# Cross attention of a two-layer block: two row normalisations move from VectorE to ScalarE, with their shift computed on GpSimd

## The chip, the cores and the metric

The kernel runs on one core of a Trainium2 chip. The metric is the device time of one execution in microseconds, of which the median over several runs is compared. In the names of the profile PE is TensorE (PEld its weight loads), DVE is VectorE, ACT is ScalarE, POOL is GpSimd and SP the engine that issues the DMAs.

## The reference, cut to what matters

The input `x` has 32 batches of 64 rows of 256 values, 2,048 rows in all. Four sublayers follow each other, each adding its output to `x`: linear attention, a mixture-of-experts feed-forward layer, softmax cross attention over `ctx_2048`, and a dense feed-forward layer. The change lies in the third. What it computes, of each row:

```
x = x + L1_xattn(_layernorm(x), ctx_2048, mask, Wq, bq, Wk, bk, Wv, bv, Wo, bo, ln_gamma, ln_beta, residual_scale)

_layernorm(x):                 (x - mean) / sqrt(var + 1e-5)
in L1_xattn:                   q, k, v projections, scores, clip, softmax, probs @ v -> ctx
delta = clip(residual_scale, 0, 0.3) * (ctx @ Wo.T + bo)
delta = (delta - mean(delta)) / sqrt(var(delta) + 1e-5) * ln_gamma + ln_beta
```

So each row is normalised twice in this layer: `x` before the query projection, and the delta before it is scaled by gamma and added to `x`.

## The kernel before, in words

The 2,048 rows are 16 tiles of 128 rows; `x` stays in SBUF for the whole run. The program has four stages, one for each sublayer. Every engine has its own instruction list, written out by hand, and the lists meet only through semaphores: `after(eng, sem, t, back)` waits until step `t - back` of `sem` is done. An engine works strictly in the order of its list, so that a waiting instruction holds back all that stands behind it.

In a stage each engine's list is a row of slots, one for each tile (`slots`, L99). Slot `s` holds work on several tiles at once: `s.tile(2)` is the tile two ahead, `s.tile(-2)` the one two behind. The first and last slots are unrolled and those between are a loop of two slots, an even and an odd one. The two differ: the queries and keys of two tiles are computed in the even slot.

In the cross attention stage (`slot2` of each engine) this happens in a slot `s`:

- PE: in an even slot the keys of two tiles (12 products), in each slot the values of tile `s` (L1342), the transpose of the attention output of tile `s-2` (L1357), in an even slot the queries of two tiles and the weighted values of tile `s-1` (L1303), then the output projection of tile `s-2` (helper lines L251 to L253), the transpose of the normalised `x` of tile `s+2` (L294), and the scores (L1326). An odd slot has the scores first and the weighted values last, behind L294.
- DVE: statistics of `x` of tile `s+2` (L266, L270), the low half of the transposed attention output (L1002), the values (L926), the normalisation of `x` of tile `s+2` (`ln_norm_step`, L286), the normalisation of the delta of tile `s-3` (`delta_norm`, L948), clipping of scores (L985), the softmax sums (L961 to L974), the delta of tile `s-2` (L935) with its statistics (L939, L943), and the low half of the transposed `x` (L307).
- ACT: in an even slot the keys (L659, four instructions), the high half of the transposed attention output (L669), in an odd slot the exponentials of the scores (L650), in an even slot the queries (L678, four), then the high half of the context (L338) and of the transposed `x` (L301), and in an odd slot L650 again.
- POOL: variance plus epsilon and its power of -1/2 of `x` of tile `s+2` (L276, L279: the reciprocal deviation, `rstd`), the low half of the context (L345), gamma, beta and the residual of tile `s-3` (L506, L508, L510), and the reciprocal deviation of the delta of tile `s-2` (L515, L518, `rstd2`).

Both normalisations are one DVE instruction each, with two values per partition as operands: subtract the mean, multiply by the reciprocal deviation. At the end of the stage slots 16 and 17 already hold work of the last sublayer: the first six of the eight feature blocks of its first group of tiles (L1287 on PE, L635 on ACT with the Gelu table), its transposes (L1272) and their copies (L645); the last two blocks follow in `slot3`.

## Time and profile before

| | us |
|---|---|
| median of 3 runs | 524.58 |
| lowest and highest run | 524.57, 527.5 |
| span of the profiled execution | 524.4 |
| PE busy in it | 485.8 (93%) |
| DVE busy | 383.4 (73%) |
| ACT busy | 217.7 (42%) |
| POOL busy | 155.0 (30%) |

The span runs from the first to the last instruction of one profiled execution; the profile gives no other time of it, and it stands 0.2 us below the median of the runs. A busy share is a mean over four stages with different limits. The cross attention stage covers roughly 327 to 453 us. Where a time point is given below, it is counted from the start of the span.

### The profile page before, as it was taken

Reading aid. Unit: us, or ns where it says so; the run is one execution under the profiler, and the core shown is the slowest. Engines: PE = TensorE matmul, PEld = TensorE weight load, DVE = VectorE, ACT = ScalarE, POOL = GpSimd, SP = SyncE. Lnnn points to the kernel's source line nnn. Section 1 sums busy time; section 2 is a strip of 40 time slices with the busy share of each in tenths; the row PEclk is TensorE's granted clock in tenths of the full one; section 3 lists DMA queues with packets and bytes.
Section 4 is the critical chain, followed back from the end, with each engine's and each line's share of the span. In section 5 each row is a group of like instructions: output and inputs, shape, how many; then the busy total and the mean of one; then the engine's idle time right before and its main releaser. Section 6 shows DMA issues by size and latency. Waiting matters only on the chain. (4 is left out here: it accounts for less than half of the span.)

```text
span 524.4 us, 11913 instructions
## 1 busy us (share of the span) xinstructions
PE 485.8 (93%) x3744; PEld 426.8 (81%) x3744; DVE 383.4 (73%) x1159; ACT 217.7 (42%) x501; POOL 155.0 (30%) x287
## 2 busy tenths in 40 slices
PE   3789999998999999999999999998899889699996
PEld 2567777776888888888888888887888878699995
DVE  5578777777777777777777776788788698666542
ACT  4444555542333333333333335553555444454540
POOL 3434444432111111111111121246455465632100
PEclk9999999999999999999999999998999799899999
DMA  8522222111000000000000000000000000000111
GB/s 279 166 57 62 58 58 58 38 41 45 16 17 16 15 15 15 15 15 15 15 15 15 16 11 11 21 22 22 12 19 20 10 1 2 0 22 22 40 40 42
DMA packets 15088, 18.06 MB, mean 34 GB/s; under 512 B 2001, under 2 KB 14546, under 8 KB 15058
## 3 DMA queue, kind: packets, MB, share of 16 engines
q1 hardware_dynamic: 15058, 17.69, 11.3%
q8 instruction: 15, 0.25, 0.2%
q14 instruction: 15, 0.12, 0.1%
HBM read 15.59 MB, written 2.10 MB: 34 GB/s over the span
## 5 line engine op out<-in xcount | busy, mean ns | idle before, releaser
L251 PE MATMUL PS<-wfh,arena_r 128*128 128x256 f32 (+2 forms) x352 | 121.3, 345 | 1.4 <-DVE arena_r L855 1.4
L252 PE MATMUL PS<-wfl,arena_r 128*128 128x256 f32 (+2 forms) x352 | 116.1, 330 | 0.0
L253 PE MATMUL PS<-wfh,arena_r 128*128 128x256 f32 (+2 forms) x352 | 116.1, 330 | 0.0
L276 POOL TENSOR_TENSOR ve<-mv,eps 128x1 f32<-128x1 f32 x64 | 12.8, 201 | 221.3 <-DVE mv L270 221.0
L251 PEld LDWEIGHTS PS<-wfh,arena_r 128*128 128x128 f32 x352 | 66.6, 189 | 10.1 <-DVE arena_r L855 4.8
L253 PEld LDWEIGHTS PS<-wfh,arena_r 128*128 128x128 f32 x352 | 66.6, 189 | 7.2
L252 PEld LDWEIGHTS PS<-wfl,arena_r 128*128 128x128 f32 x352 | 66.6, 189 | 4.9
L592 ACT ACTIVATE arena_r<-PS 128x512 fp32r<-128x512 f32 (+1 forms) x48 | 25.1, 526 | 62.2 <-PE PS L1187 62.2
L597 ACT ACTIVATE arena_f<-PS 128x512 f32<-128x512 f32 (+1 forms) x48 | 25.3, 527 | 53.0 <-PE PS L253 52.8
L286 DVE TENSOR_SCALAR arena_f<-x,mv,rstd 128x256 f32 (+1 forms) x48 | 37.0, 771 | 13.7 <-POOL rstd L279 13.3
L874 DVE SCALAR_TENSOR_TENSOR arena_f<-arena_f,tiny,PS 128x128 f32<-128x128 f32 x144 | 43.2, 356 | 0.6
L635 ACT ACTIVATE arena_f<-PS,cols 128x256 f16<-128x256 f32 x64 | 26.6, 471 | 32.4 <-PE PS L1287 30.1
L855 DVE TENSOR_TENSOR arena_r<-PS,arena_r 128x512 fp32r<-128x512 f32 (+1 forms) x48 | 28.2, 588 | 16.0 <-ACT arena_r L592 16.0
L279 POOL TENSOR_TENSOR rstd<-ve,mhalf 128x1 f32<-128x1 f32 x64 | 35.4, 552 | 8.1 <-POOL ve L276 6.0
L345 POOL TENSOR_TENSOR arena_r<-ctx_raw,arena_r 128x256 fp32r<-128x256 f32 x32 | 24.6, 770 | 43.2 <-ACT arena_r L338 43.1
L251 PE MATMUL PS<-w0h,arena_r 128*128 128x256 f32 (+1 forms) x96 | 35.0, 364 | 1.3 <-DVE arena_r L812 0.7
L1287 PE MATMUL PS<-arena_r,w1h 128*128 128x256 f32 x128 | 33.3, 298 | 2.0 <-ACT arena_r L645 1.0
L294 PE MATMUL PS<-ident,arena_f 128*128 128x128 f32 x96 | 19.6, 287 | 16.5 <-DVE arena_f L286 12.6
L358 POOL TENSOR_TENSOR wfl<-raw,wfh 128x482 f32 (+1 forms) x16 | 19.6, 1225 | 49.5 <-ACT wfh L352 49.5
L301 ACT ACTIVATE arena_r<-PS 128x256 fp32r<-128x256 f32 x48 | 18.3, 382 | 37.3 <-PE PS L294 34.3
L1287 PE MATMUL PS<-arena_r,w1l 128*128 128x256 f32 x128 | 32.8, 293 | 0.0
L1303 PEld LDWEIGHTS PS<-arena_f 128*64 128x64 f32 x512 | 30.4, 148 | 2.5 <-issue 1.5
(137 smaller groups left out, 1245.2 us busy)
## 6 DMA issues: line engine op xcount, KB each, us to landing
ctx_raw<-in_ctxT SPq DMA_DIRECT2D x32, 128.0 KB, 2.1
raw<-in_w_ffn SPq DMA_DIRECT2D x16, 241.0 KB, 2.6
raw<-in_w_l SPq DMA_DIRECT2D x16, 192.0 KB, 2.4
out<-arena_f SPq DMA_DIRECT2D x8, 256.0 KB, 2.2
x<-in_x SPq DMA_DIRECT2D x1, 1792.0 KB, 9.9
raw<-in_w_l SPq DMA_DIRECT2D x2, 512.0 KB, 5.0
rows<-in_rows SPq DMA_DIRECT2D x1, 640.0 KB, 6.1
x<-in_x SPq DMA_DIRECT2D x1, 256.0 KB, 2.8
```

What stands on the lines that cost most here:

```text
L251: nc.tensor.matmul(out_ap, lh, rh, start=first, stop=False)
L252: nc.tensor.matmul(out_ap, lh, rl, start=False, stop=False)
L253: return nc.tensor.matmul(out_ap, ll, rh, start=False, stop=last)
L279: nc.gpsimd.tensor_tensor(rstd[:, r:r + 1], ve[:, r:r + 1], mhalf[:, 0:1], ALU.pow).then_inc(ln_rstd, 1)
L286: nc.vector.tensor_scalar(dst[:, r, :], x[:, at_tile(t), :], mv[:, r, 0:1], rstd[:, r:r + 1], ALU.subtract, ALU.mult).then_inc(xn_ready, 1)
L592: nc.scalar.activation(fTh[:, at], PS[:, bank, 0:at.stop - at.start], ACT.Copy).then_inc(S1["hT_hi"], 1)
L597: nc.scalar.activation(fth[:, at], PS[:, bank, 0:at.stop - at.start], ACT.Tanh, scale=0.5).then_inc(S1["tanh"], 1)
L635: nc.scalar.activation(md16[:, r, n, :], PS[:, M_H + n // 2, (n % 2) * D:(n % 2 + 1) * D], ACT.Gelu, bias=cols[:, 2 * KC + n:2 * KC + n + ...
L855: nc.vector.tensor_tensor(fTl[:, at], PS[:, bank, 0:at.stop - at.start], fTh[:, at].bitcast(F32), ALU.subtract).then_inc(S1["hT_lo"], 1)
L874: last = nc.vector.scalar_tensor_tensor(out=fh[:, c], in0=fa[:, c], scalar=weight, in1=PS[:, bank, u:u + c.stop - c.start], op0=ALU.mult, ...
L1287: last = nc.tensor.matmul(PS[:, M_H + n // 2, (n % 2) * D:(n % 2 + 1) * D], m0w[w][:, c, n * P:(n + 1) * P], mX[r][:, c, :], start=c + w = ...
L1303: last = nc.tensor.matmul(PS[SEQ * b:SEQ * (b + 1), X_C, g * PVC:(g + 1) * PVC], pp[r][:, b, i, (c * 2 + j) * SEQ:(c * 2 + j + 1) * SEQ], ...
```

## The change

Both normalisations of the stage become ACT activations, `Identity` with a scale (the reciprocal deviation) and a bias (the shift) per partition: `x * rstd + shift`. The shift is `0 - mean * rstd`, and POOL computes it with two instructions on 128x1 behind each reciprocal deviation. DVE loses its two instructions per slot. The normalisation of `x` in the other stages stays on DVE; tiles 0 to 2 of this stage are normalised in the stage ahead and stay there too.

```diff
+        shift, shift2 = sb("shift", [P, 2]), sb("shift2", [P, 2])
+        zero = sb("zero", [P, 1])
...
+        def ln_shift_step(pool, t, r):
+
+            after(pool, ln_rstd, t, 0, 2 * TILES)
+            nc.gpsimd.tensor_tensor(shift[:, r:r + 1], mv[:, r, 0:1], rstd[:, r:r + 1], ALU.mult).then_inc(ln_mr, 1)
+            after(pool, ln_mr, t, 0, -3)
+            nc.gpsimd.tensor_tensor(shift[:, r:r + 1], zero[:, 0:1], shift[:, r:r + 1], ALU.subtract).then_inc(ln_shift, 1)
+
+        def ln_scale_step(act, t, r, dst):
+
+            after(act, ln_shift, t, 0, -3)
+            after(act, xT_psum, t, 2, 2 * TILES)
+            nc.scalar.activation(dst[:, r, :], x[:, at_tile(t), :], ACT.Identity, bias=shift[:, r:r + 1],
+                                 scale=rstd[:, r:r + 1]).then_inc(xn_ready, 1)
...
             def slot2(s):
                 if tile := normalised_in(s):
                     ln_rstd_step(pool, 2, *tile)
+                    ln_shift_step(pool, *tile)
...
                     nc.gpsimd.tensor_tensor(rstd2[:, r:r + 1], ve2[:, r:r + 1], mhalf[:, 0:1],
                                             ALU.pow).then_inc(S2["d_rstd"], 1)
+                    after(pool, S2["d_rstd"], t)
+                    nc.gpsimd.tensor_tensor(shift2[:, r:r + 1], mv2[:, r, 0:1], rstd2[:, r:r + 1],
+                                            ALU.mult).then_inc(S2["d_mr"], 1)
+                    after(pool, S2["d_mr"], t)
+                    nc.gpsimd.tensor_tensor(shift2[:, r:r + 1], zero[:, 0:1], shift2[:, r:r + 1],
+                                            ALU.subtract).then_inc(S2["d_shift"], 1)
...
                     nc.scalar.activation(aTh[:, r, :], PS[:, X_T, D:2 * D], ACT.Copy).then_inc(S2["cnT_hi"], 1)
+                if tile := s.tile(-3):
+                    t, r = tile
+                    after(act, S2["d_shift"], t)
+                    after(act, x_done[2], t, 2)
+                    nc.scalar.activation(dn[:, r, :], dl[:, r, :], ACT.Identity, bias=shift2[:, r:r + 1],
+                                         scale=rstd2[:, r:r + 1]).then_inc(S2["dn"], 1)
                 if s.ring == 1 and s.tile(-1):
                     exp_scores(*s.tile(-1))
+                if ahead := normalised_in(s):
+                    ln_scale_step(act, *ahead, xn if s.tile(2) else mx16)
                 if s.ring == 0 and s.tile(0):
...
-            slots(act, TILES, 0, TILES + 1, slot2)
+            slots(act, TILES, 0, TILES + 2, slot2)
...
-            def delta_norm(t, r):
-                after(dve, S2["d_rstd"], t)
-                after(dve, x_done[2], t, 2)
-                nc.vector.tensor_scalar(dn[:, r, :], dl[:, r, :], mv2[:, r, 0:1], rstd2[:, r:r + 1],
-                                        ALU.subtract, ALU.mult).then_inc(S2["dn"], 1)
...
                 if here:
                     values(*here)
-                if ahead:
-                    ln_norm_step(dve, 2, *ahead, xn if s.tile(2) else mx16)
-                if tile := s.tile(-3):
-                    delta_norm(*tile)
```

What this does to the lists is seen in the loop of the stage. ACT, the even slot, from the keys to the context, before:

```order
L659 ACTIVATE arena_f<-PS,bkm,headmask 128x2x2x64 x4
L118 REGISTER_ALU x2
L669 ACTIVATE arena_r<-PS 128x256
L678 ACTIVATE raw<-PS,bqm,headmask 128x2x2x64 x4
L330 ISA
```

And ACT at the same place in the changed kernel (L684 is the keys, L694 the high half of the attention output, L711 the queries):

```order
L684 ACTIVATE arena_f<-PS,bkm,headmask 128x2x2x64 x4
L118 REGISTER_ALU x2
L694 ACTIVATE arena_r<-PS 128x256
L118 REGISTER_ALU x2
L699 ACTIVATE arena_f<-arena_f,shift2,rstd2 128x256
L118 REGISTER_ALU
L295 ISA
L295 ACTIVATE arena_f<-x,shift,rstd 128x256
L711 ACTIVATE raw<-PS,bqm,headmask 128x2x2x64 x4
L347 ISA
```

Both normalisations (L699 of the delta, L295 of `x`) now stand between the attention output and the queries, and so ahead of the context step that POOL waits for.

POOL in the loop, from the residual of tile `s-3` into the next slot, before:

```order
L510 TENSOR_TENSOR x<-x,arena_f 128x256
L118 REGISTER_ALU
L515 TENSOR_TENSOR ve2<-mv2,eps 128x1
L518 TENSOR_TENSOR rstd2<-ve2,mhalf 128x1
L118 REGISTER_ALU
L276 TENSOR_TENSOR ve<-mv,eps 128x1
L118 REGISTER_ALU
```

And POOL at the same place in the changed kernel:

```order
L529 TENSOR_TENSOR x<-x,arena_f 128x256
L118 REGISTER_ALU
L534 TENSOR_TENSOR ve2<-mv2,eps 128x1
L537 TENSOR_TENSOR rstd2<-ve2,mhalf 128x1
L540 TENSOR_TENSOR shift2<-mv2,rstd2 128x1
L543 TENSOR_TENSOR shift2<-zero,shift2 128x1
L118 REGISTER_ALU
L279 TENSOR_TENSOR ve<-mv,eps 128x1
L118 REGISTER_ALU
L282 TENSOR_TENSOR rstd<-ve,mhalf 128x1
L287 TENSOR_TENSOR shift<-mv,rstd 128x1
```

Four instructions on one column are new in each slot: two for the delta ahead of the next tile's reciprocal deviation, and two (L287 and L289) behind it.

## Rows read from the trace of the kernel before

**Rows 1.** The page: granted TensorE clock in 40 slices of the span, tenths of full speed.
```profile
PEclk9999999999999999999999999998999799899999
```

**Rows 2.** Windows: stretch, length, busy us (instructions) of PE, PEld, DVE, ACT, POOL, granted clock, DMA share, GB/s.
```profile
360.00:364.00 4.00, 3.02 (x32) 2.65 (x31) 3.89 (x9) 1.63 (x4) 2.87 (x4) 0.73 0.13 33
...
408.00:412.00 4.00, 2.94 (x29) 2.41 (x27) 3.89 (x8) 1.55 (x4) 2.68 (x5) 0.70 0.11 33
...
456.00:460.00 4.00, 2.98 (x17) 2.62 (x15) 2.92 (x5) 1.38 (x4) 3.24 (x6) 0.50 0.00 0
```

**Rows 3.** Timeline of PE in an odd slot: start us, us, engine, line, [idle before].
```profile
392.27 0.39 PE L251 MATMUL PS<-w1h,arena_r 128*128 128x256 f32 x1 [0.62 <-DVE arena_r L1002]
...
394.31 0.44 PE L294 MATMUL PS<-ident,arena_f 128*128 128x128 f32 x2 [1.06 <-DVE arena_f L286]
```

**Rows 4.** Timeline of DVE, an even slot's normalisation, then an odd slot's work.
```profile
386.94 0.41 DVE L286 TENSOR_SCALAR arena_f<-x,mv,rstd 128x256 f32 x1
...
392.14 1.19 DVE L926 TENSOR_TENSOR arena_f<-PS,rows 64x128 f32<-64x128 f32 x4
393.36 0.90 DVE L286 TENSOR_SCALAR arena_f<-x,mv,rstd 128x256 f32 x1
```

**Rows 5.** Timeline of ACT, one even slot.
```profile
383.05 1.93 ACT L659 ACTIVATE arena_f<-PS,bkm,headmask 128x256 f32<-128x256 f32 x4 [1.16 <-PE PS L253]
384.86 0.39 ACT L669 ACTIVATE arena_r<-PS 128x256 fp32r<-128x256 f32 x1
385.34 1.93 ACT L678 ACTIVATE raw<-PS,bqm,headmask 128x256 f32<-128x256 f32 x4
387.15 0.43 ACT L338 ACTIVATE arena_r<-ctx_raw 128x256 fp32r<-128x256 f32 x1
```

**Rows 6.** Timeline of POOL, from the even slot's context step into the odd slot.
```profile
387.73 0.72 POOL L345 TENSOR_TENSOR arena_r<-ctx_raw,arena_r 128x256 fp32r<-128x256 f32 x1 [2.61 <-ACT arena_r L338]
...
391.10 0.55 POOL L518 TENSOR_TENSOR rstd<-ve,mhalf 128x1 f32<-128x1 f32 x1
391.99 0.19 POOL L276 TENSOR_TENSOR ve<-mv,eps 128x1 f32<-128x1 f32 x1 [0.34 <-DVE mv L270]
392.34 0.55 POOL L279 TENSOR_TENSOR rstd<-ve,mhalf 128x1 f32<-128x1 f32 x1 [0.16 <-POOL ve L276]
393.38 0.72 POOL L345 TENSOR_TENSOR arena_r<-ctx_raw,arena_r 128x256 fp32r<-128x256 f32 x1 [0.49 <-ACT arena_r L338]
```

**Rows 7.** Groups by line: two operands per partition on ACT.
```profile
L678 ACT ACTIVATE raw<-PS,bqm,headmask 128x256 f32<-128x256 f32 x25 | 12.1, 562 | 1.2 <-PE PS L253 1.0
```

**Rows 8.** Timeline of DVE, the normalisation of other odd slots.
```profile
360.47 0.82 DVE L286 TENSOR_SCALAR arena_f<-x,mv,rstd 128x256 f32<-128x256 f32 x1
...
378.14 0.89 DVE L286 TENSOR_SCALAR arena_f<-x,mv,rstd 128x256 f32 x1
...
408.59 0.90 DVE L286 TENSOR_SCALAR arena_f<-x,mv,rstd 128x256 f32 x1
...
426.62 0.90 DVE L286 TENSOR_SCALAR arena_f<-x,mv,rstd 128x256 f32 x1
```

**Rows 9.** Timeline of ACT and POOL in slots 16 and 17, where the last sublayer begins.
```profile
446.59 0.55 POOL L279 TENSOR_TENSOR rstd<-ve,mhalf 128x1 f32<-128x1 f32 x1
...
456.49 0.55 POOL L518 TENSOR_TENSOR rstd<-ve,mhalf 128x1 f32<-128x1 f32 x1
...
456.47 0.84 ACT L635 ACTIVATE arena_f<-PS,cols 128x256 f16<-128x256 f32 x2 [4.85 <-PE PS L1287]
457.20 0.66 ACT L645 ACTIVATE arena_r<-PS 128x256 fp32r<-128x256 f16 x2
```

**Rows 10.** Timeline of PE at the same place.
```profile
452.46 0.39 PE L251 MATMUL PS<-w1h,arena_r 128*128 128x256 f32 x1 [1.70 <-DVE arena_r L1002]
...
454.39 0.55 PE L1287 MATMUL PS<-arena_r,w1h 128*128 128x256 f32 x1 [0.95 <-DVE arena_f L935]
...
457.91 0.58 PE L1287 MATMUL PS<-arena_r,w1h 128*128 128x256 f32 x1 [1.02 <-ACT arena_r L645]
```

4 lines of the change are left out of this document (3 added, 1 removed).

## The prediction, made before the changed kernel ran

> **What bounds the kernel now.** I read the page first. Its busy shares give PE 93%, but that is a mean over four stages, and the change touches one of them. The line of the granted TensorE clock [rows 1] shows tenths below 9 in three places behind the middle, all at or behind 340 us: inside the cross attention stage and at its end. The windows there give the level: 0.50, the 1.2 GHz level of the two, and a mean of 0.73 or 0.70 where a window of 4 us holds the change of level [rows 2]: a clock that halves at about 361.8 and 409.6. So PE is the bound where it runs, and the stage loses time in two ways: PE pauses, and PE at half clock.
>
> The timeline of PE in the stage shows where it pauses: in the odd slots alone, once for 0.62 us until DVE has split the attention output (L1002) and once for 1.06 us until the normalised `x` of the tile two ahead is there (L286) [rows 3]. What ends the second pause is the object of this change. DVE starts L286 late, because the values (L926, four of them) stand ahead of it and end at about 393.33, and L286 then takes 0.90 us, where the same instruction in the even slot takes 0.41 [rows 4]. POOL had `rstd` ready at 392.34 + 0.55 = 392.89 [rows 6], so POOL had 0.44 us in hand there. It had 0.34 us more in front of L276, where it waited for the statistics [rows 6].
>
> The odd slot's L286 starts at 360.47, 378.14, 393.36, 408.59 and 426.62 [rows 8]. A pair of slots takes 15.22 us, and 17.67 and 18.03 us in the two pairs that hold a stretch at half clock. Such a stretch costs 2.45 and 2.81 us, 2.6 in the mean.
>
> **What the change does, part by part.** *DVE.* It loses L286 and L948 in each slot, some 0.41 + 0.41 us in an even and 0.90 + 0.4 in an odd one. In the even slot nobody waits for them. In the odd slot the end of L286 releases PE, so what counts is when the ACT instruction that takes its place ends.
>
> *One ACT normalisation.* Before, ACT has no instruction with two operands per partition that reads SBUF. The nearest row is L678, with both a bias and a scale per partition, from PSUM: 0.562 us [rows 7]. Four in a row take 1.93 us [rows 5], so one more behind another adds (1.93 - 0.562) / 3 = 0.456. Below, 0.41 (what DVE takes for it) would be a gain of 0.15 on it; above, 0.65. I take 0.56, since two operands per partition are what the two forms share. The Trainium skill, "ScalarE: Activation LUTs", "What ACT_TABLE_LOAD costs", has 186 ns plus 0.833 ns for each column plus some 93 ns for each such operand, which for 256 columns gives an estimate of 0.585 us; by it each pair of slots would be 0.05 to 0.07 us longer, 0.4 in the sum.
>
> *ACT in the even slot.* The keys, the attention output (L669, 384.86) and the queries (L678, 385.34) stand close: with the overlap of 0.10 that neighbours show, L678 could have started at 385.15, so ACT has 0.19 us in hand [rows 5]. Two normalisations put there take 0.91, so the queries and the context step behind them (L338, 387.15) come 0.72 later. POOL's L345 waits for exactly that: it had idled 2.61 us for it [rows 6].
>
> *POOL.* From L345 on POOL runs with next to no gap: L506, L508, L510, L515, L518, up to 391.65. The chain therefore moves 0.72 as a whole. Then come two instructions for `shift2`. One on a single column takes 0.19 us as L276 does, and with its wait for its predecessor 0.27 (L279 in the unrolled part starts 0.27 behind L276, 0.35 in the loop [rows 6]); two cost 0.54. They eat the 0.34 in hand. So `rstd` is ready at 392.89 + 0.72 + 0.54 - 0.34 = 393.81, and the shift at 394.35. ACT starts at 394.40 and ends at 394.96, where L286 ended at 394.26. PE's transposes come 0.70 us later, and so does all that follows, the next even slot's keys included, which releases the ACT chain of the next pair: the loop is closed, so that the 0.70 is paid again in each pair.
>
> Odd slots with this wait: those of tiles 1, 3, ..., 13, seven. 7 x 0.70 = **4.9 us**. With 0.35 for each new POOL instruction instead of 0.27 it is 0.32 more in each pair, 2.2 us in all; I keep that for the range.
>
> *The end of the stage.* In slot 16 the two normalisations stand ahead of the load of the Gelu table, which followed L669 directly. The shift that the second needs is there at 446.59 + 0.55 + 0.54 = 447.68 [rows 9], in time, so they cost 2 x 0.46 = 0.92. The last output projection (452.46), which hangs through L1002 on ACT's work behind the Gelus, moves with it. The hidden products at 454.39 waited for DVE's delta (L935) [rows 10], which stood behind L286; I take 0.25 for that wait, which goes, so they come at about 455.05. Behind them POOL has, for the last tile's delta, to run L506 to L510, L515, L518 and the two new ones. It ended L518 at 456.49 + 0.55 = 457.04 [rows 9]. Now two more pairs of shift instructions stand ahead of the chain, where POOL had waited for L948; I take 0.2 for what of them shows: 457.04 + 0.2 + 0.54 = 457.8 for the last shift. Now it matters who waits: before, this went to DVE; now ACT's last normalisation stands ahead of the two late Gelus (456.47 before) and the copies (457.20, 0.66 long). They end at 457.85 + 0.46 + 0.73 + 0.66 = 459.7 instead of 457.86 [rows 9], and PE's next products (457.91 [rows 10]) wait for the copies: **1.9 us**. Behind that the last stage is PE alone on the chain of waits, and gives nothing back.
>
> *The clock.* Both stretches at half clock in the loop begin within 0.6 us behind the end of an odd slot's pause: the pause ends with L286 at 361.29 and 409.49 [rows 8], the clock halves at about 361.8 and 409.6 [rows 2]. At the other five odd slots the same pause passes at full clock. With 1.06 + 0.70 us the second pause of every odd slot is longer by two thirds, and PE's share of the work in it lower. I expect more of the odd slots to be followed by 1.2 GHz: the trace has two in seven, all seven is the end of the scale. I take five, three more than now: 3 x 2.6 = **7.8 us**. No row says which; zero and five more (13 us) are the bounds.
>
> **The sum.** 4.9 + 1.9 + 7.8 = 14.6 us on the profiled span of 524.4 gives 539.0; the median of the runs stands 0.2 above that span, so **539 us**, +2.8%.
>
> **Rivals.** *The lists get longer, but the clock doesn't fall more often.* For it: five of seven pauses of 1.06 us passed without a fall. Against it: all of them grow. 4.9 + 1.9 = 6.8, with the falls at other places: 531.5, and 533.7 with the dearer POOL steps. Chance 0.20.
>
> *Slack takes it.* If ACT's and POOL's new work finds room that the one pair read here doesn't show (DVE is freed of 1.3 us in the odd slot, so that L270 and L1002 may come earlier and with them L276), only the end's 1.9 and part of the rest is left: 526.5. Against it: in the pair read POOL waited for ACT in the even slot, and DVE has no part in that. Chance 0.10, all of it within 1%.
>
> *DVE was held up by POOL, and that is what ends.* The odd slot's L286 overlaps POOL's L345 (393.38 to 394.10) and ends 0.16 behind it, after 0.90 us; alone it takes 0.41 [rows 4, 6]. On ACT it would take 0.56 and end at 393.36 + 0.56 = 393.92, 0.34 earlier, if the shift is there by 393.3. Then 7 x 0.34 = 2.4 us are gained; the pause until L1002 (0.62) goes too, since the odd slot's DVE list is shorter, another 0.5 x 7 = 3.5; and with shorter pauses the two half-clock stretches may go, 5.2. That gives 524.6 - 11 = 513.5 at best, 518.7 without the clock. It decides as soon as ACT's two insertions delay L345 by less than 0.2 us instead of 0.72. Against it is the 0.19 us in hand. The Trainium skill, "SBUF — State Buffer", "Who interferes with whom", has it that a VectorE tensor_scalar in its two-port mode and a GpSimd instruction shut each other out for a whole instruction, while ScalarE waits for nobody; by that rule moving the normalisation off DVE is right in itself, and the trace's 0.90 against 0.41 agrees. Chance 0.06.
>
> That leaves 0.64 for the forecast.
>
> **Numbers.** About 1% (5.2 us) is what a measurement of this kernel can tell from no change. Slower by more than that, above 529.8: forecast and first rival, 0.84. Within 1%: 0.10. Faster: 0.06. Range: the lower end reaches into the slack case at 529; the upper one is five more falls and dearer POOL steps, 524.6 + 4.9 + 2.2 + 1.9 + 13 = 546.6, so 547. About 0.1 is left out below and 0.05 above.
>
> **What would show it.** In the profile after: POOL's context step in even slots starts 0.7 us later behind the queries; POOL runs without a gap from there to the odd slot's second shift instruction; PE's transposes in odd slots wait for the ACT normalisation, about 1.8 us instead of 1.06; pairs without a fall take some 15.9 us; ACT's new instructions take 0.56; DVE idles more and is waited for less; stretches at 0.50 follow most odd slots. I am wrong if the pair stays at 15.2 (slack), if the transposes wait for ACT not because of POOL's shift but of the exponentials ahead of it, or if the half-clock stretches stay at three, in which case the sum is 7.8 too high.

## The result and the profile after

| | before | changed |
|---|---|---|
| median, us | 524.58 | 543.88 |
| lowest and highest run, us | 524.45, 527.5 (4 runs) | 540.23, 545.66 (4 runs) |
| span of the profiled execution, us | 524.4 | 543.7 |
| its mean granted clock | 0.978 | 0.948 |

The change makes the kernel slower: the ratio is 1.034, 95% interval 1.029 to 1.039. The four runs of the changed kernel took 545.5, 545.7, 542.2 and 540.2 us, the last two at a higher mean clock (0.955 and 0.961). The profiled one is the first, so its span of 543.7 is one of the two longest. The ratios here and below leave out runs more than 1.5% above the fastest of their kernel, which are three of one kernel (the normalisation of `x` on ACT in odd slots, 530.8 to 531.5 us).

The time of a run stands 1.8 us above the span of its own execution (545.53 and 543.7). By that the span of 524.4 before belongs to an execution of about 526.2 us, an estimate. So the difference of the two spans, 19.3 us, compares two executions in the upper part of their ranges; that the medians also differ by 19.3 is a coincidence.

In the program names after the change, L295 is the ACT normalisation of `x`, L699 that of the delta, L287 and L289 are POOL's shift of `x`, L540 and L543 its shift of the delta. L311 is the transpose of `x` on PE, L254 the first product of the output projection, L675 the exponentials, L355 and L362 the context step on ACT and POOL. The trace writes `shift` and `rstd` for `shift2` and `rstd2` too.

First the page: busy time and share by engine, and the granted clock in 40 slices.

```profile
PE 499.0 (92%) x3744; PEld 440.0 (81%) x3744; DVE 368.7 (68%) x1126; ACT 233.5 (43%) x534; POOL 168.1 (31%) x354
...
PEclk9989999999999999999999997998878878789999
```

ACT and POOL have grown by 15.8 and 13.1 us, DVE has lost 14.7. None of them is near full. What has changed in shape is the clock line: against three slices below 9 in the second half of [rows 1], there are now ten. (A slice of 8 between 27 and 41 us lies in the first stage; the transposes at the start of the cross attention stage come 0.36 us later than before, 327.03 against 326.67.) Three windows of 4 us from there give the level: 0.50, the 1.2 GHz level, and in two of them PE is busy for all of the 4 us.

```profile
404.00:408.00 4.00, 4.00 (x19) 4.00 (x20) 1.67 (x7) 1.05 (x3) 2.74 (x9) 0.50 0.00 0
457.00:461.00 4.00, 4.00 (x33) 3.93 (x32) 2.09 (x9) 0.90 (x1) 1.86 (x6) 0.50 0.01 4
472.00:476.00 4.00, 2.50 (x12) 2.17 (x12) 2.18 (x6) 0.70 (x2) 2.98 (x7) 0.50 0.00 0
```

Over the whole of 320 to 500 us the mean granted clock was 0.94 before and is 0.86 now. A mean of 0.94 over 180 us is 2 x 0.06 x 180 = 22 us at half clock; 0.86 is 50 us. The columns are as in [rows 2].

```profile
320.00:500.00 180.00, 164.24 (x1627) 152.70 (x1626) 133.62 (x382) 88.90 (x190) 79.08 (x155) 0.94 0.05 16
```
```profile
320.00:500.00 180.00, 157.47 (x1466) 146.21 (x1465) 107.90 (x320) 96.55 (x203) 87.51 (x209) 0.86 0.05 13
```

Next the timeline of PE at the odd slots' transposes of `x`, which answers to [rows 3]. In brackets stands the pause ahead of it and what ended it.

```profile
332.74 0.44 PE L311 MATMUL PS<-ident,arena_f 128*128 128x128 f32 x2 [1.70 <-ACT arena_f L295]
...
350.06 0.41 PE L311 MATMUL PS<-ident,arena_f 128*128 128x128 f32 x2 [0.84 <-issue]
...
365.92 0.44 PE L311 MATMUL PS<-ident,arena_f 128*128 128x128 f32 x2 [2.39 <-ACT arena_f L295]
...
380.07 0.39 PE L254 MATMUL PS<-w1h,arena_r 128*128 128x256 f32 x1 [0.26 <-DVE arena_r L1027]
...
383.33 0.44 PE L311 MATMUL PS<-ident,arena_f 128*128 128x128 f32 x2 [2.28 <-ACT arena_f L295]
...
400.97 0.44 PE L311 MATMUL PS<-ident,arena_f 128*128 128x128 f32 x2 [2.49 <-ACT arena_f L295]
...
419.36 0.69 PE L311 MATMUL PS<-ident,arena_f 128*128 128x128 f32 x2 [1.70 <-ACT arena_f L295]
...
438.39 0.44 PE L311 MATMUL PS<-ident,arena_f 128*128 128x128 f32 x2 [2.48 <-ACT arena_f L295]
...
455.97 0.29 PE L1293 MATMUL PS<-ident,raw 128*128 128x128 f16 x2 [0.66 <-ACT raw L295]
```

The pause for `x` was 1.06 us and is 2.3 to 2.5 in four of the six that ACT ends, and 1.70 in the first and at 419.36; the smaller one before it has shrunk from 0.62 to 0.26. One pair, 350.06 to 365.92, shows no loss of clock: it takes 15.86 us, where the same pair took 14.93 before. The others take 17.3 to 19.0.

ACT shows what the pause consists of. Here is its odd slot:

```profile
381.11 0.60 ACT L699 ACTIVATE arena_f<-arena_f,shift,rstd 128x256 f32<-128x256 f32 x1 [1.97 <-POOL shift L543]
381.62 1.04 ACT L675 ACTIVATE arena_f<-arena_f 128x1024 f32<-128x1024 f32 x1
382.68 0.60 ACT L295 ACTIVATE arena_f<-x,shift,rstd 128x256 f32 x1
```

And POOL from its context step in an even slot to the shifts of the odd one, one pair of slots later; it answers to [rows 6]:

```profile
394.25 0.73 POOL L362 TENSOR_TENSOR arena_r<-ctx_raw,arena_r 128x256 fp32r<-128x256 f32 x1 [4.34 <-ACT arena_r L355]
...
397.63 0.55 POOL L537 TENSOR_TENSOR rstd<-ve,mhalf 128x1 f32<-128x1 f32 x1
398.25 0.19 POOL L540 TENSOR_TENSOR shift<-mv,rstd 128x1 f32<-128x1 f32 x1
398.52 0.19 POOL L543 TENSOR_TENSOR shift<-zero,shift 128x1 f32<-128x1 f32 x1
```

From the context step on, POOL has no gap to L543 but 0.2 us ahead of L529. ACT idles for that shift of the delta, 1.97 us in the slot shown and 2.02 a pair later, and all that stands behind L699 in its list has idled with it: the exponentials and the normalisation of `x` that PE needs. The three follow each other without a gap. This closes the ring that the prediction drew: the even slot of ACT (answering to [rows 5]) holds both normalisations between keys and queries, and its context step, which POOL waits for, comes later.

```profile
388.78 1.94 ACT L684 ACTIVATE arena_f<-PS,bkm,headmask 128x256 f32<-128x256 f32 x4 [3.65 <-PE PS L256]
390.60 0.40 ACT L694 ACTIVATE arena_r<-PS 128x256 fp32r<-128x256 f32 x1
390.86 0.62 ACT L699 ACTIVATE arena_f<-arena_f,shift,rstd 128x256 f32<-128x256 f32 x1
391.35 0.61 ACT L295 ACTIVATE arena_f<-x,shift,rstd 128x256 f32 x1
391.85 1.95 ACT L711 ACTIVATE raw<-PS,bqm,headmask 128x256 f32<-128x256 f32 x4
393.64 0.45 ACT L355 ACTIVATE arena_r<-ctx_raw 128x256 fp32r<-128x256 f32 x1
```

The context step comes 4.86 us behind the keys, before 387.15 - 383.05 = 4.10 [rows 5].

At the end of the stage, answering to [rows 10], the last output projection, the first late products and the products behind the copies:

```profile
470.11 0.39 PE L254 MATMUL PS<-w1h,arena_r 128*128 128x256 f32 x1 [2.35 <-DVE arena_r L1027]
472.20 0.55 PE L1308 MATMUL PS<-arena_r,w1h 128*128 128x256 f32 x1 [0.67 <-DVE arena_f L968]
477.23 0.58 PE L1308 MATMUL PS<-arena_r,w1h 128*128 128x256 f32 x1 [2.53 <-ACT arena_r L670]
```

The last of them stands 19.3 us later than in [rows 10], and the span is 19.3 us longer. So all but 0.4 us of the loss is made between 327 and 477 us, and nothing is given back behind it.

### The profile page after: what moved, and what is told of

It reads as the page before. It is cut to its first block, busy times and chain, and to the rows that moved or that the text cites. A ratio compares the mean times of both kernels' runs of the same rounds, so it can differ in the third digit from the quotient of the medians.

```text
span 543.7 us, 11987 instructions
## 1 busy us (share of the span) xinstructions
PE 499.0 (92%) x3744; PEld 440.0 (81%) x3744; DVE 368.7 (68%) x1126; ACT 233.5 (43%) x534; POOL 168.1 (31%) x354
## 3 DMA queue, kind: packets, MB, share of 16 engines
q1 hardware_dynamic: 15058, 17.69, 10.7%
## 4 chain that ended last, share of the span: by engine, by line
PE 67%; POOL 10%; issue 8%; ACT 7%; DVE 4%; DMA 1%; ACTq 0%; POOLq 0%; SPq 0%; DVEq 0%
PE PS L254 15%; PE PS L255 14%; PE PS L256 14%; PE PS L1308 6%; PE PS L1417 6%; PE PS L1324 3%; PE PS L1208 3%; ACT raw L711 2%; POOL wfl L375 2%; PE PS L311 2%; DVE arena_f L303 1%; POOL rstd L282 1%; POOL arena_f L527 1%; POOL arena_r L362 1%; POOL arena_f L525 1%
## 5 line engine op out<-in xcount | busy, mean ns | idle before, releaser
L254 PE MATMUL PS<-wfh,arena_r 128*128 128x256 f32 (+2 forms) x352 | 121.3, 345 | 1.4 <-DVE arena_r L888 1.4
L254 PEld LDWEIGHTS PS<-wfh,arena_r 128*128 128x128 f32 x352 | 66.5, 189 | 10.1 <-DVE arena_r L888 4.8
L362 POOL TENSOR_TENSOR arena_r<-ctx_raw,arena_r 128x256 fp32r<-128x256 f32 x32 | 24.9, 777 | 53.7 <-ACT arena_r L355 53.7
L311 PE MATMUL PS<-ident,arena_f 128*128 128x128 f32 x96 | 19.8, 289 | 23.0 <-ACT arena_f L295 13.0
L1308 PE MATMUL PS<-arena_r,w1h 128*128 128x256 f32 x128 | 35.4, 310 | 3.2 <-ACT arena_r L670 2.5
L303 DVE TENSOR_SCALAR arena_f<-x,mv,rstd 128x256 f32 (+1 forms) x35 | 28.3, 810 | 13.8 <-POOL rstd L282 13.8
L254 PE MATMUL PS<-w0h,arena_r 128*128 128x256 f32 (+1 forms) x96 | 35.4, 369 | 1.4 <-DVE arena_r L845 0.8
L1308 PE MATMUL PS<-arena_r,w1l 128*128 128x256 f32 x128 | 34.7, 305 | 0.0
L1324 PEld LDWEIGHTS PS<-arena_f 128*64 128x64 f32 x512 | 32.5, 156 | 2.5 <-issue 1.5
L1324 PE MATMUL PS<-arena_f 128*64 128x34 f32 x512 | 34.4, 242 | 0.0
```

The costliest lines, as they stand in the source:

```text
L254: nc.tensor.matmul(out_ap, lh, rh, start=first, stop=False)
L303: nc.vector.tensor_scalar(dst[:, r, :], x[:, at_tile(t), :], mv[:, r, 0:1], rstd[:, r:r + 1], ALU.subtract, ALU.mult).then_inc(xn_ready, 1)
L311: last = nc.tensor.transpose(PS[:, bank, c * P:(c + 1) * P], xn[:, r, c * P:(c + 1) * P], ident[:, :])
L362: nc.gpsimd.tensor_tensor(cTl[:, :, at], ctx_raw[:, r, :].rearrange("p (c t) -> p c t", c=KC), cTh[:, :, at].bitcast(F32), ALU.subtract).t ...
L1308: last = nc.tensor.matmul(PS[:, M_H + n // 2, (n % 2) * D:(n % 2 + 1) * D], m0w[w][:, c, n * P:(n + 1) * P], mX[r][:, c, :], start=c + w = ...
L1324: last = nc.tensor.matmul(PS[SEQ * b:SEQ * (b + 1), X_C, g * PVC:(g + 1) * PVC], pp[r][:, b, i, (c * 2 + j) * SEQ:(c * 2 + j + 1) * SEQ], ...
```

## Experiments

Each was timed beside the kernel before on the same chip. Such a session has its own median of the kernel before (526.05, 526.33, 525.26 and 526.55 us in the four), so the ratios are compared, not the microseconds.

### One normalisation at a time

**The row alone on ACT:** the changed kernel without the delta's activation and its two shift instructions; DVE has `delta_norm` back.

```diff
-                    nc.gpsimd.tensor_tensor(shift2[:, r:r + 1], mv2[:, r, 0:1], rstd2[:, r:r + 1],
...
-                    nc.scalar.activation(dn[:, r, :], dl[:, r, :], ACT.Identity, bias=shift2[:, r:r + 1],
...
+                if tile := s.tile(-3):
+                    delta_norm(*tile)
```

> Only the normalisation of x is on ScalarE; the delta is normalised on VectorE as before, and GpSimd computes one shift per slot instead of two. Theory A (what holds the odd slot is ScalarE's list: the delta's activation waits for GpSimd's shift2, and the exponentials and the normalisation of x stand behind it): most of the 19.3 us goes; the pair of slots without a half-clock stretch falls from 15.9 to about 15.1, and half-clock stretches get fewer; 526 to 531 us. Theory B (the volume of GpSimd's small instructions): half of them are left, so half of the loss, 533 to 536 us. Theory C (any ScalarE normalisation of x is later than VectorE's by its longer duration, 0.60 against 0.41): 538 us or more.

Measured: 529.86 us (527.27 to 531.36, 10 runs), ratio 1.0066 (1.0025 to 1.0108).

**The delta alone on ACT:** the reverse, `ln_norm_step` back on DVE.

```diff
-                if ahead := normalised_in(s):
-                    ln_scale_step(act, *ahead, xn if s.tile(2) else mx16)
...
+                if ahead:
+                    ln_norm_step(dve, 2, *ahead, xn if s.tile(2) else mx16)
```

> Only the normalisation of the delta is on ScalarE; x is normalised on VectorE as before. Theory A: the exponentials still wait for shift2, but the transposes of x no longer stand behind them, so TensorE is released by VectorE as before; VectorE has 0.4 us less to do and its odd-slot normalisation may no longer overlap GpSimd's context step (0.41 instead of 0.90): 516 to 526 us. Theory B: half of the loss stays, 533 to 536 us.

Measured: 522.78 us (521.25 to 525.75, 10 runs), ratio 0.9946 (0.9913 to 0.9978), so half a per cent faster than before.

The one half costs 0.7%, the other gains 0.5%, and both together cost 3.4%. The effects don't add, and not in the lists either: a pair of slots at full clock takes 15.28 us with the row alone (364.55 to 379.83) and 14.77 with the delta alone (360.44 to 375.21), against 15.22 before; what it takes with both is read below, from a run at full clock. With the delta alone, DVE's normalisation of `x` in the odd slots of the loop no longer starts together with POOL's context step and takes 0.41 us instead of 0.90, as in the next two kernels that gain. With the row alone, L295 has no L699 ahead of it and waits for POOL's own chain:

```profile
379.18 0.60 ACT L295 ACTIVATE arena_f<-x,shift,rstd 128x256 f32 x1 [1.11 <-POOL shift L289]
```

Only with both does the normalisation that PE waits for stand behind one that waits for POOL. A second reading is that each half alone fits into what ACT and POOL had in hand and both together don't. The runs on the order on ACT and on POOL's chain, below, bear on this.

### The added work without its waits

**POOL's four instructions alone:** the kernel before, with the shifts computed and used by nobody.

```diff
                 if tile := normalised_in(s):
                     ln_rstd_step(pool, 2, *tile)
+                    ln_shift_step(pool, *tile)
```
(and the two of `shift2` behind the power of the delta, as in the change)

> The kernel before, with the four small GpSimd instructions of each slot added and nobody reading what they compute. Theory B (volume on GpSimd): slower than before, 0.54 - 0.34 = 0.2 us to 1.1 us a pair of slots, 526 to 533 us and more if the clock falls more often. Theory A: no loss worth speaking of, since GpSimd had 0.34 us in hand ahead of L276 and 0.44 behind L279, and a later context step no longer collides with VectorE's odd-slot normalisation: 517 to 526 us.

Measured: 523.46 us (520.09 to 524.92, 10 runs), ratio 0.9944 (0.9905 to 0.9983).

**ACT's two instructions alone:** the kernel before, with two activations a slot at the places of L699 and L295, which read a constant row and write a tile that nobody reads.

```diff
+                    nc.scalar.activation(spare[:, r, :], rows[:, 4, :], ACT.Identity, bias=eps[:, 0:1],
+                                         scale=eps[:, 0:1]).then_inc(S2["spare"], 1)
                 if s.ring == 1 and s.tile(-1):
                     exp_scores(*s.tile(-1))
+                    nc.scalar.activation(spare[:, 2 + r, :], rows[:, 4, :], ACT.Identity, bias=eps[:, 0:1],
+                                         scale=eps[:, 0:1]).then_inc(S2["spare2"], 1)
```

> The kernel before, with two ScalarE activations of the new form and size added in each slot at the places of the two normalisations; they read constants, write a spare tile and wait for nothing but themselves. Theory A: ScalarE's volume alone is nearly free, since it idles 2 us in the odd slot: 518 to 526 us. A rival (ScalarE's 0.72 us in the even slot, which delay GpSimd's context step, are what costs): 0.3 to 0.7 us a pair, 528 to 533 us.

Measured: 519.9 us (518.71 to 522.43, 4 runs), ratio 0.9881 (0.9799 to 0.9963).

This was the surprise of the study: useless work, the same in amount as what the change adds to ACT (0.59 to 0.62 us each), makes the kernel faster. With four runs the interval is wide, 0.4 to 2.0%. The timeline of DVE and then of POOL with the ACT work alone shows how. It answers to [rows 4] and [rows 6].

```profile
389.74 0.41 DVE L287 TENSOR_SCALAR arena_f<-x,mv,rstd 128x256 f32 x1
```
```profile
389.13 0.55 POOL L280 TENSOR_TENSOR rstd<-ve,mhalf 128x1 f32<-128x1 f32 x1 [0.16 <-POOL ve L277]
390.25 0.80 POOL L346 TENSOR_TENSOR arena_r<-ctx_raw,arena_r 128x256 fp32r<-128x256 f32 x1 [0.57 <-ACT arena_r L339]
```
```profile
375.46 0.44 PE L295 MATMUL PS<-ident,arena_f 128*128 128x128 f32 x2 [0.58 <-DVE arena_f L287]
...
390.20 0.44 PE L295 MATMUL PS<-ident,arena_f 128*128 128x128 f32 x2 [0.57 <-DVE arena_f L287]
```

In the odd slot DVE's normalisation now runs from 389.74 to 390.15, and POOL's context step starts at 390.25, behind it. Before, POOL started 0.02 us behind DVE, and DVE took 0.90 us for the same instruction [rows 4, 6]. The extra activation ahead of ACT's context step has pushed POOL out of DVE's way. PE's pause goes from 1.06 to 0.57, and the pair of slots from 15.22 to 14.74. With POOL's work alone the pause is 0.57 too, from the slot at 379.87 on:

```profile
394.15 0.41 DVE L296 TENSOR_SCALAR arena_f<-x,mv,rstd 128x256 f32 x1
```
```profile
394.35 0.80 POOL L355 TENSOR_TENSOR arena_r<-ctx_raw,arena_r 128x256 fp32r<-128x256 f32 x1
```

So 0.2 us of lag are enough. The slot at 362.70 of the same kernel has POOL 0.08 behind DVE, and there DVE takes 0.96 us. This is the overlap that the prediction named in its third rival. The rule of the Trainium skill that it cited for it ("SBUF — State Buffer", "Who interferes with whom", that the two shut each other out for a whole instruction, the one that issues first ahead) agrees in part. DVE takes 0.90 us where the two start together and ends 0.16 behind POOL. But there DVE started 0.02 ahead and was the one held up, and with a lag of 0.2 the two still overlap by 0.21 us, and DVE takes its usual 0.41 and POOL 0.80 instead of 0.72. What the rival had wrong is how the overlap ends: a later POOL is enough, and the normalisation may stay on DVE.

### The order on ACT, and the length of POOL's chain

**The delta's activation later:** the changed kernel with L699 moved behind the context step, so that neither the exponentials nor the normalisation of `x` stands behind it.

```diff
-                    nc.scalar.activation(dn[:, r, :], dl[:, r, :], ACT.Identity, bias=shift2[:, r:r + 1],
-                                         scale=rstd2[:, r:r + 1]).then_inc(S2["dn"], 1)
                 if s.ring == 1 and s.tile(-1):
...
                     ctx_hi_step(act, 1, *tile, S2["v_psum"])
+                if tile := s.tile(-3):
...
+                    nc.scalar.activation(dn[:, r, :], dl[:, r, :], ACT.Identity, bias=shift2[:, r:r + 1],
+                                         scale=rstd2[:, r:r + 1]).then_inc(S2["dn"], 1)
```

> The changed kernel, with the delta's activation moved in ScalarE's list from ahead of the exponentials to behind the context step, in both kinds of slot. Everything else, GpSimd's four instructions included, is as in the changed kernel. Theory A (head of the line: shift2 holds the exponentials and the normalisation of x): in the odd slot the exponentials run beside GpSimd's chain, and the normalisation of x waits for its own shift; the pause of TensorE falls from 2.4 to about 1.9 us, a pair without half clock from 15.9 to 15.4; the half-clock stretches may stay as they are many; 532 to 541 us. Theory B (volume on GpSimd): no change, 541 to 546 us.

Measured: 538.15 us (536.42 to 539.27, 4 runs), ratio 1.0212 (1.0145 to 1.0279). The pauses that ACT ends lie between 1.69 and 2.52 us in the loop, where about 1.9 was expected.

**The shift in one instruction:** the changed kernel with `mean * rstd * -1` in one POOL instruction instead of two.

```diff
-            nc.gpsimd.tensor_tensor(shift[:, r:r + 1], mv[:, r, 0:1], rstd[:, r:r + 1], ALU.mult).then_inc(ln_mr, 1)
-            after(pool, ln_mr, t, 0, -3)
-            nc.gpsimd.tensor_tensor(shift[:, r:r + 1], zero[:, 0:1], shift[:, r:r + 1], ALU.subtract).then_inc(ln_shift, 1)
+            nc.gpsimd.tensor_scalar(shift[:, r:r + 1], mv[:, r, 0:1], rstd[:, r:r + 1], -1.0, ALU.mult,
+                                    ALU.mult).then_inc(ln_shift, 1)
```

> The changed kernel, with each shift computed by one GpSimd instruction, mean * rstd * -1, instead of two. 0.27 us less ahead of shift2 and 0.27 less behind rstd. Theory A: the odd slot's chain is POOL to shift2, the delta's activation, the exponentials, the normalisation of x, which holds only shift2's saving: 0.27 us a pair, 2 us in all, plus what the clock makes of it: 537 to 543 us. Theory B: both count, 0.54 a pair, 4 us: 534 to 541 us.

Measured: 538.94 us (534.06 to 540.82, 4 runs), ratio 1.0207 (1.0117 to 1.0297). Both theories allowed that, so the time alone doesn't decide between them.

**Both together:**

> Both together: the delta's activation behind the context step and one GpSimd instruction for each shift. Theory A: the chains to the odd slot's normalisation of x are both short, a pair takes 14.8 to 15.2 us as before or less, with three to five half-clock stretches: 520 to 532 us. If only the volume counts: as the kernel with one instruction for each shift.

Measured: 534.3 us (533.18 to 538.13, 4 runs), ratio 1.0125 (1.0058 to 1.0192). That is above the 520 to 532 expected.

Each of the two gives back some 1.3 points of the 3.4, and both give back 2.1 (the interval of the one-instruction shift just touches that of the change, 1.0286 to 1.0394). What they do to the lists is seen in pairs of slots at full clock. With the delta's activation later, such a pair runs from 380.52 to 396.94:

```profile
380.52 0.44 PE L311 MATMUL PS<-ident,arena_f 128*128 128x128 f32 x2 [1.70 <-ACT arena_f L295]
...
396.94 0.54 PE L311 MATMUL PS<-ident,arena_f 128*128 128x128 f32 x2 [2.52 <-ACT arena_f L295]
```

That is 16.42 us, no less than the 16.4 that the next section finds for the changed kernel at full clock. L295 has nothing of the delta ahead of it any more, but waits for POOL's shift L289 itself, 2.20 us in that odd slot and 0.62 in the even one before it, where it holds up the queries: the context step comes 5.15 us behind the keys (384.49 and 389.64). With the one-instruction shift two such pairs take 15.97 and 15.98 (383.03 to 399.00, 417.46 to 433.44). In the second pair it is the other way round: 15.86 in the changed kernel, 15.50 with the delta's activation later (346.65 to 362.15), 15.73 with the one-instruction shift (348.98 to 364.71). The changed kernel's odd slot above fits that: the chain over L699 and the exponentials and the chain through POOL's second shift arrive there within 0.22 us of each other. To shorten one of them leaves the other. How much of each 1.3 points is lists and how much is clock (0.91 and 0.90 instead of 0.86), no run separates.

In the third the ACT timeline shows L294, here the normalisation of `x`, ahead of L712, the delta's, and it still waits for POOL's shift:

```profile
380.10 0.60 ACT L294 ACTIVATE arena_f<-x,shift,rstd 128x256 f32 x1 [1.53 <-POOL shift L287]
380.61 0.40 ACT L354 ACTIVATE arena_r<-ctx_raw 128x256 fp32r<-128x256 f32 x1
380.91 0.59 ACT L712 ACTIVATE arena_f<-arena_f,shift,rstd 128x256 f32<-128x256 f32 x1
```

So the place of L699 is not all of it. With it out of the way, POOL's chain itself is the last to arrive, since ACT's even slot still delays its start (the context step comes 4.37 us behind the keys, 353.98 and 358.35, where it was 4.10). The pauses for `x` stay at 1.5 to 1.85 us, the second and third pair of slots are at 15.19 and 15.53 (350.03, 365.22 and 380.75 on PE), some 0.65 us less than in the changed kernel at full clock (15.83 and 16.17, next section) and still 0.3 more than before, and the clock is little better than with the change: 0.89 over 320 to 500 us. That is of an execution of 538.13 us, the slowest of the four of this kernel. The expectation had taken the pause to fall to about what it was before, and the clock with it.

**The normalisation of `x` on ACT in odd slots alone**, with the one-instruction shift, the rest as before. The even slot of ACT is then free of both.

```diff
+                if s.ring == 1 and (ahead := normalised_in(s)):
+                    ln_scale_step(act, s.pair, *ahead, xn if s.tile(2) else mx16)
...
-                if ahead:
+                if ahead and even:
                     ln_norm_step(dve, 2, *ahead, xn if s.tile(2) else mx16)
```

> The kernel before, with only the normalisation of x in odd slots on ScalarE (behind the exponentials), its shift by one GpSimd instruction; even slots and the delta stay on VectorE. Theory A: the shift is ready at 392.89 + 0.27 = 393.16, the activation ends at 393.21 + 0.60 = 393.81, where VectorE ended at 394.26: 0.45 us a pair gained, 3 us in all, and shorter pauses may spare the two half-clock stretches, 5 us more: 516 to 522 us. Rival (VectorE was not what held the odd slot): 524 to 526 us.

Measured: 527.17 us (522.91 to 531.54, 12 runs), ratio 1.0019 (0.9985 to 1.0052): no difference, and above the 516 to 522 expected. The idea was that on ACT the instruction could not be held up by POOL's context step.

```profile
378.52 0.60 ACT L293 ACTIVATE arena_f<-x,shift,rstd 128x256 f32 x1 [0.62 <-POOL shift L286]
```

It is not held up, but it costs 0.60 us instead of 0.41 (0.90 with the overlap), and it has one more step of POOL ahead of it: `rstd` was ready at 377.87, the shift at 378.31, and ACT started at 378.52. That is 0.65 us after `rstd`, and 1.25 from `rstd` to the end. Before, it was 1.37 (392.89 to 394.26 [rows 4, 6]), so 0.12 us are gained where 0.45 were expected. The expectation had put the shift 0.27 us behind `rstd` and ACT 0.05 behind the shift; measured are 0.44 and 0.21. What ACT gains in the collision it loses on the way. PE waited 6.6 us for it in six odd slots, before 6.4.

### The clock alone

**The changed kernel with its pauses filled:** 14 matmuls whose result nobody reads (128x128 by 128x256, on a weight that lies in SBUF anyway) ahead of the transposes in each odd slot. This is more work for PE and no less for anyone.

```diff
                         after(pe, S2["cnT_lo"], before[0])
+                    if s.ring == 1:
+                        after(pe, xT_lo, tile[0], 1, 2 * TILES)
+                        for _ in range(14):
+                            nc.tensor.matmul(PS[:, X_T, 0:D], m0w[0][:, 0, 0:P], m0w[0][:, 0, 0:D], start=True,
+                                             stop=True)
                     transpose_x(pe, 2, *tile, X_T)
```

> The changed kernel, with 14 products of 128x256 on constants, 1.7 us of TensorE work whose output is overwritten, put into the odd slot's pause of 2.4 us, ahead of the transposes of x. They lengthen no chain while they are shorter than the pause. Theory (the half-clock stretches follow from TensorE's pauses, and cost 0.38 us for each us at half clock, as the two in the loop of the kernel before do): the stretches of the loop go, some 34 us of half clock, 13 us: 529 to 533 us. Rival (the stretches come from something else, or cost nothing since other engines hold the pair): 542 to 547 us.

Measured: 530.59 us (529.73 to 531.27, 10 runs), ratio 1.0069 (1.0041 to 1.0098), as expected. Of the 3.4% of the change 2.7 points are gone, some 14 us. Not all of that is a price of the change, since the kernel before gains from the same filling too (0.7 points, by the kernel after this one). PE, an odd slot of the loop and then the page's clock line and the windows:

```profile
376.81 1.83 PE L1396 MATMUL PS<-w1h 128*128 128x256 f32 x14
379.46 0.44 PE L311 MATMUL PS<-ident,arena_f 128*128 128x128 f32 x2 [0.82 <-ACT arena_f L295]
```
```profile
PEclk9999999999999999999999999999999999789999
```
```profile
320.00:500.00 180.00, 166.38 (x1692) 155.71 (x1692) 117.15 (x341) 103.74 (x221) 89.84 (x217) 0.97 0.05 16
```

The transposes still wait for L295, so the added matmuls stand in the pause and hide no wait. Only the clock has changed: no slice of the loop is below 9. The pairs are now as long as the lists make them at 2.4 GHz: 15.0, 15.8, 16.2, and then 16.4 us three times, ahead of the last, shorter one.

**The kernel before with its pauses filled** by six such matmuls:

> The kernel before, with 6 products of 128x256 on constants, 0.75 us, put into the odd slot's second pause of 1.06 us. If pauses make the half-clock stretches and each of the two in the loop costs 2.6 us: 519 to 520 us. If not: 524 to 527 us.

Measured: 521.59 us (520.92 to 522.96, 11 runs), ratio 0.9930 (0.9902 to 0.9957), 1.6 us above what was expected. The two stretches at half clock in the loop are gone, the pair stays at 15.24. So the kernel before too paid for its pauses twice.

**The odd slots' ACT normalisation, filled** likewise with six:

> The two together: x of odd slots on ScalarE and 6 products on constants in the odd slot's pause. If the pause is now 0.6 us, the 0.75 us of filling may show with 0.1 to 0.2 us a pair, 1 us in all: 517 to 520 us.

Measured: 521.03 us (520.49 to 521.55, 6 runs), ratio 0.9912 (0.9879 to 0.9945) and 1 us above the 517 to 520 expected. The pauses of this kernel could be filled as well as those of before, but it has no advantage over that one beyond what the intervals allow. Its pair takes 15.11 us (376.18 to 391.29), against 15.24.

**The delta alone on ACT, filled** with five. This is the half of the change that pays, together with the filling that keeps the clock up:

> The delta's normalisation alone on ACT (as in the run that measured 522.8 us), with five matmuls whose result nobody reads (128x128 by 128x256) added in the pause of PE in each odd slot of the stage, ahead of the transposes that wait for DVE's normalisation of x. Theory: the pause of 0.80 to 0.85 us holds five of them (six took 0.70 to 0.78 us of a pause of 1.06 in the earlier run), so the pairs keep their length, and the half clock at the start of the tail, 17.1 us of it in that run, shrinks to the one stretch of 10 to 13 us that the filled kernels had: 4 to 7 us less at half clock, 1.5 to 2.7 us less in time, so 520 to 521.5 us. Rival: the pauses of 0.8 us did not cost any clock in that kernel, its fall lies behind the stage where nothing is filled, and the extra work delays the transposes slightly: 522.5 to 524 us.

Measured: 520.33 us (519.75 to 521.57, 6 runs), ratio 0.9875 (0.9853 to 0.9898). The theory holds: the clock of 320 to 500 us rises from 0.95 to 0.97 and the pair takes 14.77 us. The four fastest versions (this one, the useless ACT work, and the two filled ones above) lie between 0.988 and 0.993. The interval of this one (to 0.9898) just ends below that of the kernel before, filled (from 0.9902); between the others the runs don't decide.

### All of them side by side

The wait is what PE waited for the normalised `x` in the transposes between 330 and 465 us in the profiled execution (six odd slots in most, five to seven in the filled ones), the clock is the mean of 320 to 500 us in it. The ratio is of all runs, so a row joins one execution with a median.

| kernel | wait for `x`, us | clock | ratio |
|---|---|---|---|
| ACT work alone | 4.0 | 0.96 | 0.988 |
| delta on ACT, filled | 1.5 | 0.97 | 0.988 |
| odd rows on ACT, filled | 1.6 | 0.97 | 0.991 |
| before, filled | 2.2 | 0.97 | 0.993 |
| POOL work alone | 4.6 | 0.95 | 0.994 |
| delta on ACT | 5.3 | 0.95 | 0.995 |
| before | 6.4 | 0.94 | 1 |
| odd rows on ACT | 6.6 | 0.93 | 1.002 |
| row on ACT | 8.7 | 0.93 | 1.007 |
| after, filled | 4.5 | 0.97 | 1.007 |
| both, one-op and later | 10.0 | 0.89 | 1.013 |
| delta later | 11.4 | 0.91 | 1.021 |
| one-op shift | 11.9 | 0.90 | 1.021 |
| after | 13.0 | 0.86 | 1.034 |

In the rows that are not filled the wait and the time rise together, but for two neighbours at 1.021 that the runs can't tell apart; the clock follows with small exceptions. The filled ones leave this line: the clock is high whatever the wait.

## Why the prediction came out as it did

It said 539 us, in a range of 529 to 547, slower. Measured were 543.9. The direction, the places and both halves of the cause were right; the sum was 4.7 us too low on the profiled spans (14.6 of 19.3 us). The 0.2 us by which it put the median above the span compares unlike things, since a run's time is 1.8 above its own span; it does not touch the sum of the change. The filled kernel lets the two halves be measured apart, since it has the lists of the changed kernel at the high clock throughout the loop. Its transposes start at 332.50 in the first odd slot, its last at 443.18 (441.97 before, 455.97 after), its last output projection at 454.33 and its products behind the copies at 461.23.

| term | predicted | measured |
|---|---|---|
| first odd slot of the loop | 0 | 0.7 (332.50 against 331.83) |
| seven pairs, lists alone | 4.9 | 5.8 (332.50 to 443.18 is 110.68; 331.83 to 441.97, less the 5.26 of its two falls, is 104.88) |
| end of the stage, lists alone | 1.9 | 2.1 (11.15 + 6.90 against 10.49 + 5.45) |
| clock | 7.8 | 10.7 (the rest of 19.3) |

That the filling itself delays nothing in the first odd slot, where no pause is left in front of L311, is not shown; it can have added 0.1 us there.

**The pair of slots: mechanism right, size too small.** The chain was the one described: two activations ahead of the queries, POOL's context step later, POOL without a gap, two more instructions, ACT, PE. The context step came 0.76 us later behind the keys where 0.72 was said, and a pair without a fall 15.86 us where 15.9 was said. That agreement is luck, since that one pair was still using up slack of the start of the loop. With the clock high throughout, the pair settles at 16.4, which is 1.2 more than the 15.22 of before, not 0.70. Over the seven pairs this makes 5.8 us for 4.9, since the first and the last grow by less. In the prediction POOL's chain and its shift lead straight to ACT's normalisation of `x`; it left out what stands between. ACT's L699, which waits for the first of POOL's two shifts, the exponentials (1.04) and L295 follow each other in ACT's list, and 0.51 + 1.06 + 0.60 us after L699 starts it is done, provided that POOL has the shift of `x` by then. In the odd slot shown POOL had the shift of `x` at 382.27 + 0.19 = 382.46, 0.22 us before ACT began with it. So the prediction's own condition for being wrong, that the transposes wait for the exponentials and not for POOL's shift of `x`, was met. In that slot it cost 0.22 us at most. The run with L699 moved away shows what then comes up behind it: L295 waits for POOL's shift L289, and a late pair at full clock takes 16.42 us, as much as in the filled kernel. With both cures the pairs are some 0.65 us shorter. So there are two chains of nearly the same length, of which the prediction counted the one through POOL, and either by itself makes a late pair of some 16 us (16.42 and 15.97). Which link makes the ring 1.2 us longer instead of 0.70 was not traced further.

**One ACT normalisation: 0.56 taken, 0.60 measured.** The group in the changed kernel:

```profile
L699 ACT ACTIVATE arena_f<-arena_f,shift,rstd 128x256 f32<-128x256 f32 x16 | 9.7, 607 | 13.7 <-POOL shift L543 13.6
L295 ACT ACTIVATE arena_f<-x,shift,rstd 128x256 f32 (+1 forms) x13 | 7.9, 607 | 0.7 <-POOL shift L289 0.6
```

It lies inside the bounds of 0.41 and 0.65. The estimate worked out from the Trainium skill, "ScalarE: Activation LUTs", "What ACT_TABLE_LOAD costs", was 0.585 and so nearer; the trace has 0.607 in the mean. The group's idle time also shows who held whom: 13.6 us of ACT's waiting stands ahead of L699 and 0.6 ahead of L295 (0.9 more in its four at the end of the stage, a group by themselves). Who stands first in the list takes the wait, so this alone doesn't say what the order costs.

**POOL's instructions:** 0.19 each and 0.27 from one to the next, as taken. The work alone, in the kernel before, costs nothing (0.9944).

**The end of the stage:** 2.1 measured against 1.9. The copies did wait for the chain as said: ACT's last L699 idled 3.52 us for POOL's last shift, ahead of the late Gelus.

```profile
475.30 0.60 ACT L699 ACTIVATE arena_f<-arena_f,shift,rstd 128x256 f32<-128x256 f32 x1 [3.52 <-POOL shift L543]
475.81 0.82 ACT L660 ACTIVATE arena_f<-PS,cols 128x256 f16<-128x256 f32 x2
476.52 0.66 ACT L670 ACTIVATE arena_r<-PS 128x256 fp32r<-128x256 f16 x2
```

**The clock: the largest term and the one most off, 10.7 us for 7.8.** This is the term that was mis-sized. I counted stretches in the loop alone, three more at 2.6 us. In the loop that was nearly the right sum (123.2 us for the seven pairs against 110.7 with the pauses filled is 12.5, less the 5.3 of before is 7.3), although the falls were neither so few nor of one size: one pair lost nothing, the other six lost between 1.2 and 3.0. What was left out is the end of the stage. From the last transposes to the last output projection the changed kernel takes 14.14 us, filled 11.15: 3.0 us go there to a stretch at 0.50, the window at 457 us above, where the kernel before had full clock until 452.46. The prediction had the pauses there grow and gave them no clock. The share of the clock holds up in another comparison: the filling takes 2.7 points from the changed kernel and 0.7 from the one before, so 2.0 points, some 10.5 us, are what the change costs by the clock.

**The rivals.** The lists without the clock: refuted by the windows, though the filled kernel is nearly that. Against the kernel before as it is it stands at 1.007, but that kernel has falls of its own; against the kernel before, filled (0.993), it is 1.014, some 7 us, and that is what the lists alone cost. The forecast for this rival, 6.8 us, was close (524.6 and 6.8 make 531.4, not 531.5). Slack takes it: only the first pairs had some. The overlap of DVE and POOL ends and the kernel gets faster: wrong for this change, because ACT's even slot delayed POOL as said; but the gain exists, and two kernels that only add work collect it. That moving the normalisation of `x` off DVE is right in itself, as the prediction has it under this rival, no run here bears out: in odd slots alone it made no difference (1.002), and in all slots it cost 0.7%. I gave this rival 0.06 and took the overlap for the smaller effect. Its size, 0.90 against 0.41 us, was stated right and never looked at as something that could be had by itself.

## What to carry to other kernels

An engine's free time does not tell what an operation costs there. What counts is the ring of waits that it joins: here ACT and POOL were less than half busy, and each move alone cost 0.7% or gained 0.5%, but both together made the ring through ACT's even slot and POOL's chain 1.2 us longer in each pair of slots. So measure two moves together, and don't add up what each costs. An instruction that waits for another engine holds up all that stands behind it in its list. But where two chains arrive almost together, as here, moving it away gives back little until the other chain is shortened too. When PE waits in short pauses, read the granted clock beside them, count the lost clock at the end of a stage too, and test with matmuls that do nothing in the pause, which costs little and tells apart what the wait and what the clock costs. And where an instruction of DVE takes twice its usual time beside one of POOL, try first to shift one of the two in time before moving it to another engine.

## What the runs showed of the hardware that was not expected

- Added work can be a gain: two useless activations a slot made the kernel 1.2% faster (0.4 to 2.0), four POOL instructions on one column 0.6% (0.2 to 1.0), and in both POOL's 128x256 instruction then starts 0.2 us or more behind DVE's instead of 0.02 (DVE then takes 0.41 us instead of 0.90; with a lag of 0.08 it took 0.96).
- PE pauses of some 2.4 us, once in a pair of slots of 16 us, brought the clock of 320 to 500 us to a mean of 0.86; 14 matmuls in 1.83 us of each pause brought it to 0.97 and the time down by 2.7 points. With pauses of 1.06 us it is 0.94, and 0.97 with six matmuls in them.
- An activation on 128x256 from SBUF with both scale and bias per partition takes 0.60 us, the same normalisation on DVE 0.41.
- The kernel before spreads by more than one set of three runs shows: over four sessions its runs lie between 522.3 (mean clock 0.986) and 530.1 us (0.970), while the filled kernels stay within 0.4%. An explanation that would fit is that whether a pause costs the clock differs from run to run; it was not tested.
